# Attention job table: a11, aT0 and a00 moved beside other jobs (steps 4 to 5, 6 to 7, 15 to 14)

## What is computed

```python
x = x + tanh(g_xattn) * xattn(layernorm(x), ctx, pos, pos, Wq, Wkv, Wout, bout)
x = x + tanh(g_ffn)   * ffn(layernorm(x), gate_w, up_w, down_w, expert_weight, gamma, beta)

# xattn: 32 heads of 16, q and k turned by an axial rotary embedding of pos
q = rope(x @ Wq); k, v = split(ctx @ Wkv); k = rope(k)
attn = softmax(q k^T / 4) v;  return attn @ Wout + bout
# ffn: h = relu(x @ up)^2; y = h @ down + (x @ expert) * (sum of the top 2 gate logits)
#      return layernorm(y) * gamma + beta
```

## Time and profile before

| | us |
|---|---|
| median of three runs | 1622.49 |
| lowest and highest | 1620.65, 1623.03 |
| the profiled execution, its own time | 1620.87 |
| its span, first to last instruction | 1619.1 |
| TensorE busy | 1562.0 (96%) |
| VectorE busy | 975.4 (60%) |
| ScalarE busy | 638.3 (39%) |
| GpSimd busy | 295.5 (18%) |

### The profile page before, as it was taken

How to read it: one execution, slowest core, us unless ns; L and a number is a source line. 1 busy time by engine, 2 the same in 40 slices (tenths; PEclk the granted TensorE clock), 3 DMA queues, 4 the chain that set the end, 5 groups by cost and what they waited for, 6 DMA issues and landing times.

```text
span 1619.1 us, 26178 instructions
## 1 busy us (share of the span) xinstructions
PE 1562.0 (96%) x9883; PEld 1166.3 (72%) x9883; DVE 975.4 (60%) x1448; ACT 638.3 (39%) x962; POOL 295.5 (18%) x370
## 2 busy tenths in 40 slices
PE   8699999999999999988999999999999999999997
PEld 6456666666666666655787887887878878788786
DVE  7587788788777778865662634436445354353524
ACT  4165555555555555566442222222222222222221
POOL 5222222222222222201000201002011020010202
PEclk9799999999999999999999999999999999999999
DMA  6624444554443444343540100101101011010101
GB/s 176 135 64 107 110 117 108 126 126 120 119 103 102 106 109 122 84 113 94 155 125 1 53 27 32 32 17 47 32 20 40 20 47 33 8 52 20 52 1 39
DMA packets 67191, 121.22 MB, mean 75 GB/s; under 512 B 12280, under 2 KB 25720, under 8 KB 67064
## 3 DMA queue, kind: packets, MB, share of 16 engines
q1 hardware_dynamic: 67064, 119.50, 27.6%
HBM read 51.17 MB, written 16.78 MB: 42 GB/s over the span
## 4 chain that ended last, share of the span: by engine, by line
PE 83%; DVE 10%; issue 2%; ACT 1%; POOL 1%; DMA 1%; SPq 1%; POOLq 0%; DVEq 0%; ACTq 0%
PE pP L984 16%; PE pA L1180 11%; PE pO L984 11%; PE pB L1180 11%; PE pT L984 9%; PE pA L1075 6%; PE pO L1103 6%; PE pM L984 4%; DVE mneg L1399 4%; PE pB L1091 2%; PE pT L991 2%; PE pM L991 2%; PE pP L991 2%; PE pM L1147 1%; DVE rot L1327 1%
## 5 line engine op out<-in xcount | busy, mean ns | idle before, releaser
L1399 DVE TENSOR_REDUCE mneg<-pA 128x4 f32<-128x1024 f32 x250 | 305.7, 1223 | 139.4 <-PE pA L1075 137.5
L887 ACT ACTIVATE probs<-pB 128x1024 f32<-128x1024 f32 x249 | 255.2, 1025 | 267.1 <-PE pB L1091 246.3
L1502 DVE TENSOR_TENSOR relu<-relu 128x512 f32<-128x512 f32 x128 | 88.3, 689 | 257.3 <-ACT hid L937 257.3
L704 POOL TENSOR_SCALAR var_eps<-meanvar 128x1 f32<-128x1 f32 x96 | 34.6, 360 | 1058.1 <-DVE meanvar L1284 1057.9
L1180 PE MATMUL pA<-dn,hid 128*128 128x512 f32 x768 | 198.8, 394 | 0.9 <-DVE hid L1504 0.2
L1180 PE MATMUL pB<-dn,hid 128*128 128x512 f32 x768 | 196.0, 390 | 0.0
L984 PE MATMUL pP<-fT,up 128*128 128x512 f32 x768 | 190.3, 396 | 0.0
L984 PE MATMUL pO<-fT,up 128*128 128x512 f32 x768 | 187.5, 393 | 0.0
L1180 PEld LDWEIGHTS pA<-dn,hid 128*128 128x128 f32 x768 | 143.1, 188 | 36.2 <-DVE hid L1504 4.8
L984 PEld LDWEIGHTS pO<-fT,up 128*128 128x128 f32 x768 | 144.4, 188 | 32.3 <-issue 0.4
L1180 PEld LDWEIGHTS pB<-dn,hid 128*128 128x128 f32 x768 | 144.2, 188 | 31.0
(11 more groups left out here) (201 smaller groups left out, 1991.5 us busy)
## 6 DMA issues: line engine op xcount, KB each, us to landing
stk<-kT SPq DMA_DIRECT2D x180, 128.0 KB, 2.9
stq<-qT SPq DMA_DIRECT2D x180, 128.0 KB, 3.0
fres<-x_scratch SPq DMA_DIRECT2D x34, 256.0 KB, 2.8
xin<-x SPq DMA_DIRECT2D x32, 256.0 KB, 2.9
xres<-x SPq DMA_DIRECT2D x32, 256.0 KB, 3.5
x_scratch<-xres SPq DMA_DIRECT2D x32, 256.0 KB, 2.4
out<-y_s SPq DMA_DIRECT2D x32, 256.0 KB, 2.0
fx<-x_scratch SPq DMA_DIRECT2D x29, 256.0 KB, 2.7
```

The costliest lines, as they stand in the source:

```text
L704: nc.gpsimd.tensor_scalar_add(var_eps[:], meanvar[:, 1:2], EPS).then_inc(ve_made, 1)
L887: nc.scalar.activation(probs[:, s % 4, :, :, :].rearrange("p a b s -> p a (b s)"), psum[:, :, :], ACT.Exp).then_inc(exp_done, 1)
L1399: nc.vector.tensor_reduce(mneg[par][:, :, 2 * u:2 * u + 2].rearrange("p t q -> p q t"), psum[:, :, :].rearrange("p q (t k) -> p q t k", t= ...
L1502: nc.vector.tensor_tensor(r[:], r[:], r[:], ALU.mult).then_inc(sq_made, 1)
```

## The change

Three jobs change their step in the table. a11 goes from step 4, where it stood alone behind times_v, to step 5, behind X1 and kT0. aT0 goes from step 6, where it stood alone behind times_v, to step 7, in front of K1 and the first half of Q1. a00 goes from step 15, where it stood alone, to step 14, behind V0. Steps 4, 6 and 15 have no job left. All three engines read the same table, so that the emptying of each moves by one step too: on VectorE a11 comes behind kT0 in step 6, aT0 in front of K1 in step 8, a00 in step 15 in front of the layer norm. Since a00 of the last item is now emptied inside the last iteration, the separate call after it is gone. The order of the jobs within each bank, the number of instructions, and every DMA stay as they were.

```diff
-    4: ("a11",),
-    5: ("X1", "kT0"),
-    6: ("aT0",),
-    7: ("K1", "Q1<"),
+    4: (),
+    5: ("X1", "kT0", "a11"),
+    6: (),
+    7: ("aT0", "K1", "Q1<"),
     8: ("Q1", "O0<"),
...
-    14: ("V0",),
-    15: ("a00",),
+    14: ("V0", "a00"),
+    15: (),
 }
...
             phase1(dve, iteration, ahead=1)
 
 
-            job("a00", B - 1)
             split_gate()
             job("a10", B)
```

## The result

| | before | after |
|---|---|---|
| median, us | 1621.97 (4 runs, 1620.65 to 1623.03) | 1648.96 (4 runs, 1646.32 to 1649.29) |
| ratio | | 1.0165, 95% interval 1.0149 to 1.0180 |
| profiled execution, its own time | 1620.87 | 1648.87 |
| its span | 1619.1 | 1647.0 |

A forecast was written before the change was run, and what follows sets the result against it. TensorE bounds the kernel, with VectorE holding it up in places; steps 4 to 7 are run by both queues. 18.3 + 6.5 + 1.0 = 25.8 us on 1620.87 gives 1646.7, plus 1.62: median 1648.3 us, range 1645 to 1652.

The forecast's parts named there:

- The floor: Every step: logits, reduction, next logits take at least 1.82 us, since pA has one buffer, however little else there is.
- a11 out of step 4, nothing gained: Steps 4 and 5: X1 still waits for VectorE to empty Q0, so the shorter step 4 gains nothing.
- a11 behind kT0, aT0's wait: Steps 5 to 7: aT0 waits 1.1 us for a11's emptying; 1.41 us lost in each of iterations 1 to 13.
- Covers: kT1 and O0's first half: aT0's later emptying stays hidden, at nothing; broken cover up to 0.6 us an iteration, chance 0.06.
- a00: Steps 14 and 15: step 14 grows, step 15 stays at 1.82 us; 0.43 us lost in each of iterations 0 to 14.
- The ends: Iteration 14: about 0 beside a00; iteration 15: O0 waits for aT0's emptying, between -1 and +3 us, taken as +1.
- The sum: Whole kernel: 13 x 1.41 + 15 x 0.43 + 1.0 = 25.8 us slower.
- The clock: Steps 5 to 7: no clock term in the sum; a fall in steps 5 to 8 gives about 1714 us, chance 0.02.
- The hidden wait: Rival, at aT0: VectorE empties a11 in time, step 8 only 0.27 us late, median 1633.5 us; chance 0.07.
- The opposite side: Rival: jobs fill holes, steps 4 to 7 gain 0.60 us, step 15's wait absorbs a00; 1615.7 us, chance 0.03.

The follow-up runs named there:

- a00_only: Only a00 moved, from step 15 to step 14 behind V0, against the kernel before: 1627.45 us, ratio 1.0034.
- cut_V0_early_norm_kT0: Kernel before with V0 halved over steps 14 and 15, layer-norm statistics in VectorE's step 13, kT0 in front of X1: 1612.39 us, ratio 0.9951.
- the cut V0: Kernel before with V0 cut in halves, one left in step 14, one put into step 15 in front of a00: 1613.09 us, ratio 0.9957.
- a11_first: Kernel before with a11 moved to step 5 in front of X1 and aT0 to step 7, a00 staying: 1635.29 us, ratio 1.0077.

## Why the prediction was right

*The floor.* Right, and used three times: the emptied steps 4, 6 and 15 are 1.82, 1.83 and 1.83 us long.

*a11 out of step 4, nothing gained.* Right: X1 starts when VectorE lets it, and its wait grew by 0.42 us, to 0.77: that is what step 4 gives up, 2.24 us (441.93 to 444.17 in the trace before) less 1.82. The 0.9 us that I had forecast for this wait do not follow from that and are too much; nothing in the sum hangs on them.

*a11 behind kT0, aT0's wait.* Right in place, releaser and size: a wait of 1.1 us was forecast, it is 1.07. Steps 4 to 7 were to take 11.85 us and take 11.79. The 0.06 are in two intervals: a11 follows kT0 after 0.44 us, where I had taken 0.49 from the pair X1 and kT0, and K1 to step 8 is 2.93 instead of 2.95. So the term is 13 x 1.35 = 17.6, not 18.3.

*Covers.* Both held: kT1 starts without a wait (472.17) behind the later rope sum, which ends at 471.79, so 0.38 us of the cover's 0.98 are left; and in iterations 1 to 13 the first half of O0 never waits.

*a00.* Right: 0.44 us an iteration in the trace of a00_only, 6.5 us by the sum, 5.6 measured alone. Iteration 15, which the sum left out for a00, also grew by 0.43 there (35.98 to 36.41).

*The ends.* Iteration 14 without a00 was put at 0 and came out at -0.05 (36.97 to 37.35 us, a00's 0.43 in it). Iteration 15 is the term that was mis-sized: I took +1 between -1 and +3, and it measured +3.1 in the profiled execution (35.98 to 39.12). The mechanism named there, aT0's emptying behind a layer norm, is the one in the trace, and the waits alone came to 1.7 us, inside the bounds; the clock's fall, 1.5 us on top of it, was a term that the sum put at nothing, with a reason given for steps 5 to 7 only.

*The sum.* The span grew by 27.9 us: 23.2 in iterations 1 to 13, 0.6 at the start with iteration 0, 0.4 in iteration 14, 3.1 in iteration 15, and 0.6 in the feed-forward part, which I did not follow up. The forecast was 25.8. The median came out closer to its forecast (1648.96 against 1648.3) than the profiled execution did (1648.87 against 1646.7), and that is luck: I had added 1.62 us for the distance between the two before, and after it is 0.09.

*The clock.* I judged that the trace of iteration 14 speaks against a fall, and for the changed kernel that holds: 1.00 in the whole of the iterations 1 to 13. In iteration 15 it fell, as said. And as a statement about steps 5 to 7 it was on thin ice: in a11_only, where a11 alone is moved, a wait of 1.92 us in each iteration cost 4.0 us of it on average, 2.2 of them by waiting and 1.8 through the clock. The rule of the Trainium skill that I had set against the row (TensorE: Matmul & The Clock Gate, "A second HAM failure mode: psum-queue depth-cycling") describes a11_only well: short waits between groups of matmuls, and a clock that swings between its two levels, here in 11 of 13 iterations.

*The rivals.* The hidden wait is excluded by the trace, where aT0 waits 1.07 us. The opposite side, holes filled and a faster kernel, is excluded by a00_only for its second half and by cut_V0_early_norm_kT0 for its first: with nothing in front of X1 the step still waits for VectorE.

## What to carry to other kernels

Before moving a job into another slot, write down what each slot is bound by, and price the emptied slot at its floor and not at the work that is left in it. Then follow the job through the other engine's list: a bank is free when that engine comes to it, so the place in that list has a price (here 0.39 us an iteration between the last and the first place in step 6), and the next user of the same bank must stand far enough behind it. Work pays where it goes into a slot at its floor and comes out of one that is full, as with the cut V0.

## What the runs showed of the hardware

The clock's sensitivity to short waits was new to me in this size: with a wait of 1.92 us in each of 13 iterations, the clock fell behind it in 11 of them; in the one shown, the granted clock was 0.53 in the 7.3 us behind the wait and a product took 2.93 us instead of 1.66. With 0.87 us of that wait filled with repeated matmuls (1.05 us were left) the clock stayed at 1.00, and the kernel became 20 us faster by doing more work. With waits of 1.07 and 0.77 us in the same steps of the changed kernel it stayed at 1.00 as well. At the end of the attention part, in iteration 15, it fell in some kernels and not in others (1.00 before, 0.84 in a11_first); what decides it there is open. Two stops of TensorE of more than 2 us, with no releaser, appeared in a part of the program that the added matmuls do not touch; their cause is open.
